# Counting a graph's edges in groups of three tiles and windows of 32 instead of five and 48

## The chip, the core and the metric

The kernel runs on one core of a Trainium2 chip. The metric is the device time of one execution in microseconds (us), lower being better. The core's engines run programs of their own and meet at semaphores: TensorE (PE) for matmuls and transposes, VectorE (DVE), ScalarE (ACT), GpSimd (POOL), and SyncE (SP), whose queue issues the DMAs. Matmuls write to PSUM, eight banks of 512 float32 columns; everything else lives in SBUF.

## The reference

Two graph attention layers over one graph of 1250 nodes and 21,250 edges (10,000 random pairs in both directions, and one loop per node), which come sorted by destination.

```
x = layernorm(x + gat0(x, src, dst))        # 12 heads of 64
x = layernorm(x + gat1(x, [src, dst]))      # 4 heads of 256, then 1 head of 768
# in each: e = leaky_relu(a1[src] + a2[dst]); w = exp(e - max over the edges of dst)
#          out[dst] = sum of w * ft[src] / sum of w, over the edges of dst
```

## The kernel before

Attention is computed densely: for every pair of nodes the kernel needs the number of edges between them, a matrix CT of 1250 x 1250 counts, held as ten tiles of 128 source nodes by 1250 destinations. Its logarithm (LC, in the same memory) is later added to the scores. So the first stage counts edges, and everything from the logarithms on waits for all counts.

**How edges are counted.** The edges make 170 tiles of 125. For each tile DVE builds two one-hot matrices: `hot_cell` (L1550, 125 edges x 480 columns) says in which of 10 x 48 cells the edge falls, the cell being the source's tile of 128 nodes and the destination's place in a window of 48 destinations; `hot_rows` (L1609, built for ten tiles in one operation, "the row op") says which of 128 rows the source is. PE multiplies the two (L759), and the product adds the tile's edges to a PSUM bank of 128 x 480 counts. Five tiles (GT) make a group with one window, since the edges are sorted; the group's window begins at its smallest destination, the base, which is data and is loaded into a register. There are 34 groups. Groups take turns on two banks, 0 and 4.

**How a group leaves its bank.** ACT copies columns 1 to 47 of each window over CT (L1214, `keep_window`); column 0, in which neighbouring groups may both have edges, is added to CT by DVE (L1562, `add`, 128 x 10 elements). Both load the base first (L1208 on ACT, L1566 on DVE). The last group is added whole by DVE, and that sets the semaphore `counted`.

**What orders it.** Every engine's order is written out by hand. PE may begin group g when `win_added` says that the add of group g-2 is done, so that its bank is free. DVE's order in group g is: one-hot tiles 0 and 1, the add of group g-2, the load of group g-1's base, tiles 2 and on. The add waits for PE to have finished group g-2 (`win_free`) and for ACT's copy of it (`win_kept`). A one-hot tile waits for the tile ten before it to be used, as there are ten `hot_cell` buffers.

**What PE and ACT do between.** PE interleaves the counting with the first layer's other work: transposes of x (L867) in 18 turns, with copies on ACT (L1243), and projections (L895) in 20 steps, with copies on ACT (L1263, L1265); in two places also transposes of attention rows (L881, copies L1254). `x_counts` and `proj_counts` say how many counting segments stand ahead of each turn or step. A segment is three or two tiles, and stands in an `If`, as another program runs if a group's destinations are spread too far for a window. Between two pieces of other work (four turns, or two steps) stand two groups. On ACT the copies of the groups stand at the same places.

## Time and profile before

| what | us |
|---|---|
| median of 3 runs | 1126.23 |
| lowest and highest | 1125.57, 1126.36 |
| the profiled execution | 1124.05 |
| its span, first to last instruction | 1122.3 |
| counting, first one-hot tile to `counted` | 11.6 to 79.0 |

The profile is of one execution. Its own time, 1124.05, is the span and 1.75 around it. Over the whole span PE is busy 94%, DVE 85% and ACT 57%. The three thirds of the kernel have different limits, so what a change in the counting does must be read from the stretch up to 79 us and from what waits for its end.

### The profile page before, as it was taken

To read this page: it belongs to the slowest core of one execution; us is meant where nothing else is said; L and a number is where in the kernel's file an instruction comes from. 1 tells how busy PE (TensorE), PEld (TensorE's weight loads), DVE (VectorE), ACT (ScalarE), POOL (GpSimd) and SP (SyncE) were. 2 spreads that over 40 slices of the span, in tenths; PEclk is the share of its full clock that TensorE was granted. 3 is DMA by queue.
4 is the path that set the end of the run, shared out by engine and by line. 5 is a ranking of instruction groups with operands and counts; after the bars stand their busy time and mean duration, and the time that the engine had idled before them with its cause. 6 is when DMAs were issued, how large, how long until landed. Compare 5 with 4: busy or idle time off the path is not lost.

```text
span 1122.3 us, 20577 instructions
## 1 busy us (share of the span) xinstructions
PE 1052.4 (94%) x8048; PEld 905.6 (81%) x8048; DVE 952.9 (85%) x1531; ACT 642.5 (57%) x939; POOL 142.6 (13%) x155
## 2 busy tenths in 40 slices
PE   6986999898989899999999999999999999999996
PEld 4665666666666667999999999999988888888885
DVE  7989999999999999977853999999987874497865
ACT  8658999999999997223111567666612311234331
POOL 1000000000000000010073112020400153311111
PEclk9998999999999999999999999999999999999998
DMA  4061020202020205533237310204041124343211
GB/s 150 1 235 44 3 92 1 93 1 92 2 92 1 98 1 197 171 101 120 80 107 267 124 47 1 84 1 151 20 169 57 44 95 174 131 162 126 78 60 53
DMA packets 40022, 98.99 MB, mean 88 GB/s; under 512 B 4505, under 2 KB 17393, under 8 KB 39925
## 3 DMA queue, kind: packets, MB, share of 16 engines
q1 hardware_dynamic: 39926, 97.66, 24.9%
q8 instruction: 66, 1.08, 0.4%
q14 instruction: 30, 0.25, 0.1%
HBM read 70.74 MB, written 26.90 MB: 87 GB/s over the span
## 4 chain that ended last, share of the span: by engine, by line
PE 61%; DVE 20%; ACT 9%; issue 8%; DMA 1%; DVEq 1%; POOL 0%; SPq 0%; POOLq 0%; ACTq 0%
PE psum L1110 14%; PE psum L1019 13%; PE psum L1071 12%; DVE R L1692 9%; PE psum L1149 8%; DVE R L1678 5%; ACT R L1288 5%; PE psum L1034 4%; ACT R L1304 3%; PE psum L759 2%; PE psum L1087 1%; PE psum L944 1%; DVE LC L1664 1%; PE psum L1140 1%; PE psum L1122 1%
## 5 line engine op out<-in xcount | busy, mean ns | idle before, releaser
L944 PE MATMUL psum<-ident,R 128*128 128x128 f32 (+3 forms) x1200 | 156.8, 279 | 38.3 <-ACT R L1288 37.8
L944 PEld LDWEIGHTS psum<-ident,R 128*128 128x128 f32 (+3 forms) x1200 | 127.5, 142 | 78.9 <-ACT R L1288 66.5
L1692 DVE CUSTOM_DVE_ANT_0 R<-R,LC 128x1250 f32<-128x1250 f32 x120 | 175.1, 1462 | 0.2 <-DVE LC L1664 0.2
L1288 ACT ACTIVATE R<-R,row_max 128x1250 f32<-128x1250 f32 x120 | 161.6, 1347 | 2.0 <-DVE row_max L1692 1.6
L958 PE MATMUL psum<-R 128*64 128x256 f32 (+3 forms) x1200 | 147.2, 383 | 0.6 <-ACT R L1304 0.6
L1304 ACT COPY R<-psum 128x1280 f32<-128x1280 f32 x120 | 143.7, 1198 | 1.5 <-PE psum L944 1.5
L1019 PE MATMUL psum<-w_hi,x1T_hi 128*128 128x256 f32 (+1 forms) x480 | 128.6, 283 | 0.7 <-DVE x1T_lo L1784 0.7
L1019 PE MATMUL psum<-w_hi,x1T_lo 128*128 128x256 f32 (+1 forms) x480 | 127.3, 280 | 0.0
L1019 PE MATMUL psum<-w_lo,x1T_hi 128*128 128x256 f32 (+1 forms) x480 | 125.7, 281 | 0.0
L1678 DVE SCALAR_TENSOR_TENSOR R<-R 128x1250 f32<-128x1250 f32 x80 | 121.9, 1525 | 0.0
L2177 POOL TENSOR_TENSOR rstd<-rstd,minus_half 128x1 f32<-128x1 f32 (+1 forms) x40 | 33.9, 847 | 664.1 <-DVE rstd L1707 664.1
L958 PEld LDWEIGHTS psum<-R 128*64 128x64 f32 (+1 forms) x1200 | 79.0, 137 | 43.6 <-issue 10.1
L1019 PEld LDWEIGHTS psum<-w_hi,x1T_hi 128*128 128x128 f32 (+1 forms) x480 | 86.6, 186 | 1.3 <-issue 1.3
L1019 PEld LDWEIGHTS psum<-w_hi,x1T_lo 128*128 128x128 f32 (+1 forms) x480 | 86.3, 186 | 0.0
L1019 PEld LDWEIGHTS psum<-w_lo,x1T_hi 128*128 128x128 f32 (+1 forms) x480 | 85.4, 186 | 0.1
L1375 ACT CAST et_hi<-psum 128x1280 fp32r<-128x1280 f32 (+1 forms) x40 | 48.2, 1206 | 56.6 <-PE psum L1034 56.6
L1367 ACT ACTIVATE R<-R,row_max 128x1250 f32<-128x1250 f32 (+1 forms) x40 | 53.7, 1342 | 33.3 <-DVE row_max L1846 33.2
L1983 DVE TENSOR_TENSOR h1T_lo<-psum,h1T_hi 128x1024 fp32r<-128x1024 f32 (+1 forms) x18 | 21.8, 1209 | 54.8 <-ACT h1T_hi L1403 54.8
L1403 ACT CAST h1T_hi<-psum 128x1024 fp32r<-128x1024 f32 (+1 forms) x18 | 18.1, 1006 | 81.6 <-PE psum L1087 81.6
L1924 DVE TENSOR_TENSOR et_lo<-psum,et_hi 128x1280 fp32r<-128x1280 f32 (+1 forms) x40 | 58.2, 1455 | 7.1 <-ACT et_hi L1375 5.7
L1678 DVE SCALAR_TENSOR_TENSOR R<-rowbuf,R 128x1250 f32<-128x1250 f32 (+1 forms) x40 | 60.7, 1523 | 0.0
L1846 DVE CUSTOM_DVE_ANT_0 R<-R,LC 128x1250 f32<-128x1250 f32 (+1 forms) x40 | 58.7, 1468 | 0.1
(234 smaller groups left out, 2482.9 us busy)
## 6 DMA issues: line engine op xcount, KB each, us to landing
R<-rows_spill SPq DMA_DIRECT2D x20, 625.0 KB, 5.2
rowbuf<-rows_spill SPq DMA_DIRECT2D x14, 625.0 KB, 5.2
lc_spill<-LC SPq DMA_DIRECT2D x9, 625.0 KB
LC<-lc_spill SPq DMA_DIRECT2D x9, 625.0 KB, 5.6
res_spill<-colbuf SPq DMA_DIRECT2D x36, 128.0 KB, 3.3
R<-res_spill SPq DMA_DIRECT2D x9, 512.0 KB, 3.5
R<-in_x_dram SPq DMA_DIRECT2D x1, 3456.0 KB
res_spill<-R SPq DMA_DIRECT2D x9, 384.0 KB
```

What stands on the lines that cost most here:

```text
L944: last = e.transpose(turn0[r % 2][0:m, s, 0:n_dst], ring[0:n_dst, r % RING0, s * P:s * P + m], ident[0:n_dst, 0:n_dst])
L958: last = e.matmul(banks[6][k * C0:(k + 1) * C0, 0:w], x_in[0:m, s, (2 * g + k) * C0:(2 * g + k + 1) * C0], exp_bufs0[(2 * n + k) % 4][0:m, ...
L1019: last = e.matmul(gemm_bank1(p)[0:m, 0:C1], xs[:, i * KT + k, 0:m], ws[b % WBUFS1][:, k, :], start=(n == 0), stop=(n == len(steps) - 1))
L1071: last = e.matmul(acc1[r % 2][0:w, :], cols[r % 2][0:m, s, 0:w], xs[h % 2][0:m, s, :], start=(s == 0 and step == 0), stop=(s == NT - 1 and ...
L1110: last = e.matmul(acc2[v % 2][0:m, c:c + w], hs[v % 2][:, k, 0:m], ws[k][:, c:c + w], start=(k == 0 and step == 0), stop=(k == KH - 1 and ...
L1149: last = e.matmul(acc2[r % 2][0:n_dst, c:c + w], cols[r % 2][0:m, s, 0:n_dst], xs[s][0:m, c:c + w], start=(s == 0 and step == 0), stop=(s ...
L1288: e.activation(ring[0:m, r % RING0, :], ring[0:m, r % RING0, :], ACT.Exp, bias=row_max[0:m, r % RING:r % RING + 1], scale=-1.0, accum_out= ...
L1304: e.copy(exp_bufs0[(2 * n + j // 2) % 4][:, :, (j % 2) * P:(j % 2) * P + rows[i]], turn0[r % 2][:, :, 0:rows[i]]).then_inc(S.kept0, 1)
L1678: e.scalar_tensor_tensor(out=ring[0:m, r % RING0, :], in0=row_slope[0:m, :], scalar=att_part0[0:m, i, H0 + h:H0 + h + 1], in1=row[0:m, :], ...
L1692: e.tensor_tensor_reduce(slot, slot, LC[0:m, i, :], -1.0, MIN_CEILING, ALU.add, ALU.min, row_max[0:m, r % RING:r % RING + 1]).then_inc(S.l ...
L1846: e.tensor_tensor_reduce(slot1(r)[0:m, :], slot1(r)[0:m, :], LC[0:m, i, :], -1.0, MIN_CEILING, ALU.add, ALU.min, row_max[0:m, r % RING:r % ...
L1924: e.tensor_tensor(et_lo[r % 2][:, :, 0:w], turn1[r % 2][:, :, 0:w], et_hi[r % 2][:, :, 0:w].bitcast(F32), ALU.subtract).then_inc(S.et_lo, 1)
```

## The change

Groups are of three tiles, with windows of 32 destinations: 57 groups, of which the last has two tiles. A one-hot tile has 10 x 32 = 320 columns, and so has its matmul; ACT's copy has 310 elements per row. The number of `hot_cell` buffers stays ten, and the row op still makes ten tiles. A segment is now one group. Between two pieces of PE's other work stand three groups (nine tiles) instead of two (ten tiles); ahead of the first transposes seven groups (21 tiles) instead of four (20), and after the last projection eight groups (23 tiles) instead of three (15). Because 57 groups of three are not 170 tiles, the destinations that give the bases are loaded by two DMAs, and the subtraction of the bases is two operations.

```diff
-    GT = 5
-    GROUPS = ET // GT
-    WIN = 48
+    GT = 3
+    GROUPS = (ET + GT - 1) // GT
+    WIN = 32
...
-        HOT = 2 * GT
+        HOT = 10
...
-            e.dma_start(groups_i, dst.rearrange("(g e) -> g e", g=GROUPS)).then_inc(S.groups_in, 16)
+            e.dma_start(groups_i[0:KEPT, :], dst[0:KEPT * GT * EP].rearrange("(g e) -> g e", g=KEPT)).then_inc(S.groups_in, 16)
+            e.dma_start(groups_i[KEPT:GROUPS, :], dst[E - GT * EP:E].rearrange("(g e) -> g e", g=1)).then_inc(S.groups_in, 16)
...
-        def windows_pe(e, g, tiles):
-            if g >= 2 and tiles[0] == 0:
+        def group_tiles(g):
+            return range(g * GT, min(g * GT + GT, ET))
+
+        def windows_pe(e, g):
+            if g >= 2:
                 e.wait_ge(S.win_added, g - 1)
-            for j in tiles:
-                e.wait_ge(S.win_hot, g * GT + j + 1)
-                hot_row = hot_rows[g // 2 % 2][:, :, g % 2 * GT + j]
-                e.matmul(banks[4 * (g % 2)][:, 0:NT * WIN], hot_row, hot_cell[(g * GT + j) % HOT], start=(j == 0),
-                         stop=(j == GT - 1)).then_inc(S.win_free, 1)
+            tiles = group_tiles(g)
+            for t in tiles:
+                e.wait_ge(S.win_hot, t + 1)
+                hot_row = hot_rows[t // PAIR % 2][:, :, t % PAIR]
+                e.matmul(banks[4 * (g % 2)][:, 0:NT * WIN], hot_row, hot_cell[t % HOT], start=(t == tiles[0]),
+                         stop=(t == tiles[-1])).then_inc(S.win_free, 1)
...
-        SEGMENTS = [range(0, 3), range(3, GT)]
-        COUNTS = len(SEGMENTS) * GROUPS
-        W_COUNTS, FIRST_COUNTS, TURN_COUNTS = 2, 8, 26
+        W_COUNTS, FIRST_COUNTS, TURN_COUNTS, STEP = 2, 7, 22, 3
 
         def x_counts(turn):
-            return FIRST_COUNTS + turn // 4 * 2 * len(SEGMENTS)
+            return FIRST_COUNTS + turn // 4 * STEP
 
         def proj_counts(pair):
-            return TURN_COUNTS + pair // (2 * KG) * 2 * len(SEGMENTS)
+            return TURN_COUNTS + pair // (2 * KG) * STEP
...
             for g in range(GROUPS):
-                if g and g % 2 == 0:
-                    rows_of_pair(g // 2)
-                for j in range(GT):
-                    tile(g * GT + j)
+                for j, t in enumerate(group_tiles(g)):
+                    if t and t % PAIR == 0:
+                        rows_of_pair(t // PAIR)
+                    tile(t)
                     if g >= 2 and j == 1:
                         add(g - 2, base)
                     if g and j == 1:
...
-            e.tensor_tensor(by_group(dst_rel), by_group(banks[0][0:EP, 0:ET]),
-                            base_all.unsqueeze(2).to_broadcast([EP, GROUPS, GT]), ALU.subtract).then_inc(S.prep, 1)
+            for to, node, base in zip(by_group(dst_rel), by_group(banks[0][0:EP, 0:ET]), bases_by_group()):
+                e.tensor_tensor(to, node, base, ALU.subtract).then_inc(S.prep, 1)
```

PE's order in the projection stretch, from the end of the first group of a block to the next projection, before (`win_hot_ready` is set by DVE's one-hot tiles, `win_sum_added` is `win_added`):

```order
L822 UNCONDITIONAL_BRANCH
L822 COMPARE_AND_BRANCH
L759 MATMUL psum<-R 128x480 [waits win_hot_ready,win_sum_added]
L759 MATMUL psum<-R 128x480 [waits win_hot_ready] x2
L822 UNCONDITIONAL_BRANCH
L822 COMPARE_AND_BRANCH
L759 MATMUL psum<-R 128x480 [waits win_hot_ready] x2
L822 UNCONDITIONAL_BRANCH
L895 MATMUL psum<-R 128x66 [waits ft]
```

The same place after the change, from the end of the first group of a block:

```order
L825 UNCONDITIONAL_BRANCH
L825 COMPARE_AND_BRANCH
L765 MATMUL psum<-R 128x320 [waits win_hot_ready,win_sum_added]
L765 MATMUL psum<-R 128x320 [waits win_hot_ready] x2
L825 UNCONDITIONAL_BRANCH
L825 COMPARE_AND_BRANCH
L765 MATMUL psum<-R 128x320 [waits win_hot_ready,win_sum_added]
L765 MATMUL psum<-R 128x320 [waits win_hot_ready] x2
L825 UNCONDITIONAL_BRANCH
L898 MATMUL psum<-R 128x66 [waits ft]
```

A third group, with a wait of its own for an add, now stands ahead of the projection.

DVE's order around one row op, before (L1562 ISA computes an address for the add and carries its waits; `win_rest_kept` is `win_kept`, `win_hot_free` is `win_free`):

```order
L1550 TENSOR_SCALAR R<-R 125x480 [waits win_hot_free] x3
L1609 TENSOR_TENSOR R<-R 125x1280
L1550 TENSOR_SCALAR R<-R 125x480 [waits win_hot_free] x2
L1562 ISA [waits win_sum_added,win_rest_kept,win_hot_free]
L1562 TENSOR_TENSOR LC<-LC,psum 128x10
L1566 TENSOR_LOAD R
L1566 ISA x2
L1550 TENSOR_SCALAR R<-R 125x480 [waits win_hot_free] x5
```

The same after the change:

```order
L1557 TENSOR_SCALAR R<-R 125x320 [waits win_hot_free] x3
L1569 ISA [waits win_sum_added,win_rest_kept,win_hot_free]
L1569 TENSOR_TENSOR LC<-LC,psum 128x10
L1573 TENSOR_LOAD R
L1573 ISA x2
L1616 TENSOR_TENSOR R<-R 125x1280
L1557 TENSOR_SCALAR R<-R 125x320 [waits win_hot_free] x3
L1569 ISA [waits win_sum_added,win_rest_kept,win_hot_free]
```

Add, load and their waits now stand behind every three tiles instead of every five, and the row op falls at changing places in the groups.

## Rows read from the trace of the kernel before

**Rows 1.** Busy us of each engine (instructions) by stretch, granted clock, DMA
```profile
core 0: us, PE busy (x) PEld busy (x) DVE busy (x) ACT busy (x) POOL busy (x), PEclk, DMA share, GB/s
22.00:36.00 14.00, 12.95 (x87) 10.16 (x85) 14.00 (x54) 10.10 (x22) 0.00 (x0) 1.00 0.01 2
79.10:360.00 280.90, 246.78 (x2008) 179.84 (x2008) 280.60 (x297) 256.58 (x351) 0.00 (x0) 0.98 0.14 49
```

**Rows 2.** Instructions in time: start, duration, engine, operation, idle before; a projection-stretch block
```profile
45.41 2.25 PE L759 MATMUL psum<-R 125*128 125x480 bf16 x10
...
46.19 0.16 DVE L1562 TENSOR_TENSOR LC<-LC,psum 128x10 f32 x1
46.27 1.34 DVE L1550 TENSOR_SCALAR R<-R 125x480 bf16<-125x480 f16 x5
...
46.76 0.56 ACT L1214 COPY LC<-psum 128x470 f32 x1 [0.68 <-PE psum L759]
47.54 0.16 DVE L1562 TENSOR_TENSOR LC<-LC,psum 128x10 f32 x1
...
47.59 1.56 PE L895 MATMUL psum<-R 64*128 64x66 f32 x24
...
48.17 0.85 DVE L1550 TENSOR_SCALAR R<-R 125x480 bf16<-125x480 f16 x3 [0.47 <-PE psum L759]
```

**Rows 3.** The same view, the counting's start
```profile
11.98 2.21 PE L759 MATMUL psum<-R 125*128 125x480 bf16 x5 [3.46 <-DVE R L1550]
...
15.32 0.56 ACT L1214 COPY LC<-psum 128x470 f32 x1 [0.18 <-PE psum L759]
...
16.11 0.17 DVE L1562 TENSOR_TENSOR LC<-LC,psum 128x10 f32 x1 [0.65 <-PE psum L759]
...
16.76 0.60 DVE L1550 TENSOR_SCALAR R<-R 125x480 bf16<-125x480 f16 x2 [0.48 <-PE psum L759]
...
17.16 0.14 PEld L759 LDWEIGHTS psum<-R 125*128 125x128 bf16 x1 [0.32 <-DVE R L1550]
```

**Rows 4.** Waits from 16 to 79.2 us: us in total, times, longest
```profile
PEld psum L759 <- DVE LC L1562: 4.4, 10, 0.7
```

**Rows 5.** Groups by line up to 130 us: busy us, mean ns of one, idle before
```profile
L1550 DVE TENSOR_SCALAR R<-R 125x480 bf16<-125x480 f16 x170 | 47.3, 338 | 4.7 <-PE psum L759 3.4 <-issue 1.0
...
L1609 DVE TENSOR_TENSOR R<-R 125x1280 bf16<-125x1280 f16 x17 | 13.9, 819 | 0.0
```

**Rows 6.** In order of time: the transposing stretch, its first and last transposes
```profile
19.33 1.67 PE L867 MATMUL psum<-ident,R 128*128 128x128 f32 x14
...
20.06 1.82 ACT L1243 COPY R<-psum 128x512 f32<-128x512 f32 x4
...
20.84 2.20 PE L759 MATMUL psum<-R 125*128 125x480 bf16 x10
...
33.28 0.80 PE L867 MATMUL psum<-ident,R 128*128 128x128 f32 x6
```

**Rows 7.** In order of time: the first and the tenth pair of projections
```profile
36.27 1.56 PE L895 MATMUL psum<-R 64*128 64x66 f32 x24
...
71.70 1.41 PE L895 MATMUL psum<-R 64*128 64x66 f32 x24
```

**Rows 8.** In order of time: the block behind the first row transposes
```profile
57.60 2.20 PE L759 MATMUL psum<-R 125*128 125x480 bf16 x10
...
59.29 0.53 ACT L1214 COPY LC<-psum 128x470 f32 x1
```

**Rows 9.** In order of time: the end of the counting
```profile
73.04 3.24 PE L759 MATMUL psum<-R 125*128 125x480 bf16 x12
...
75.45 0.17 DVE L1562 TENSOR_TENSOR LC<-LC,psum 128x10 f32 x1
...
79.07 0.28 DVE L1757 TENSOR_SCALAR R<-att 128x240 f32<-128x240 f32 x1
```

**Rows 10.** DVE's base loads, line L1566: times, ns min/median/max, first and last start
```profile
L1566 DVEq TENSOR_LOAD <-R x34: 297/304/942, 11.8 to 76.5; - x34
```

More of the change, by code:

```diff
@@ L53, in gnn_kernel @@
     RING = 8
-    GT = 5
-    GROUPS = ET // GT
-    WIN = 48
+    GT = 3
+    GROUPS = (ET + GT - 1) // GT
+    WIN = 32
     KEPT = GROUPS - 1
     HT = NT // 2
-    assert GROUPS * GT == ET and GROUPS % 2 == 0 and NT % 2 == 0 and NT * WIN <= BANK
+    assert KEPT * GT < ET and NT % 2 == 0 and NT * WIN <= BANK
     x1_dram = nc.dram_tensor("x1_spill", (N, D), F32, kind="Internal").ap()
@@ L168, in gnn_kernel @@
         RHS_AT = NT * D + 4 * P
-        hot_at = [RHS_AT + KT * PROJ + j * (NT * WIN // 2) for j in range(GT + 1)]
-        assert hot_at[GT] <= NT * (D + XW)
-        hot_cell = [edge_view([NT * WIN], BF16, EP) for _ in range(GT)]
-        hot_cell += [view(R2, at, [NT * WIN], BF16, EP) for at in hot_at[0:GT]]
-        PAIR = 2 * GT
+        hot_at = [RHS_AT + KT * PROJ + j * (NT * WIN // 2) for j in range(HOT // 2 + 1)]
+        assert hot_at[HOT // 2] <= NT * (D + XW)
+        hot_cell = [edge_view([NT * WIN], BF16, EP) for _ in range(HOT // 2)]
+        hot_cell += [view(R2, at, [NT * WIN], BF16, EP) for at in hot_at[0:HOT // 2]]
+        PAIR = HOT
         hot_rows = [edge_view([P, PAIR], BF16, EP) for _ in range(2)]
@@ L187, in gnn_kernel @@
         groups_i = edge_view([GT * EP], I32, GROUPS)
-        assert iota_at <= 4 * N and edge_at[0] >= 6 * N
+        edge_at[0] = max(edge_at[0], 6 * N)
+        assert iota_at <= 4 * N
         hot_full = [edge_view([N], BF16, EP) for _ in range(2)]
@@ L818, in pe_program, with count_group @@
             e.sem_inc(S.all_free, 2)
-            def count_segment(n):
-                g, part = divmod(n, len(SEGMENTS))
+            def count_group(g):
                 with e.If(span < WIN):
-                    windows_pe(e, g, SEGMENTS[part])
-                if n == 0:
+                    windows_pe(e, g)
+                if g == 0:
                     with e.Else():
@@ L828, in count_segment @@
                         last.then_inc(S.win_free, ET)
-                if n == COUNTS - 1:
+                if g == GROUPS - 1:
                     with e.Else():
@@ L834, in count_until @@
                 for at in range(done, n):
-                    count_segment(at)
+                    count_group(at)
                 return max(done, n)
@@ L899, in pe_program @@
                     turn_rows(n)
-            count_until(done, COUNTS)
+            count_until(done, GROUPS)
             e.wait_ge(S.counted, 1)
@@ L1216, in keep_until @@
             def keep_until(kept, counts):
-                for g in range(kept, min(counts // len(SEGMENTS), KEPT)):
+                for g in range(kept, min(counts, KEPT)):
                     keep_window(g)
-                return max(kept, min(counts // len(SEGMENTS), KEPT))
+                return max(kept, min(counts, KEPT))
             kept = keep_until(0, W_COUNTS)
@@ L1268, in act_program @@
                     keep_rows(n)
-            keep_until(kept, COUNTS)
+            keep_until(kept, GROUPS)
             for s in range(NT):
@@ L1543, in by_group, with bases_by_group @@
         def by_group(per_tile):
-            return per_tile.rearrange("p (g t) -> p g t", t=GT)
+            return [per_tile[:, 0:KEPT * GT].rearrange("p (g t) -> p g t", t=GT), per_tile[:, KEPT * GT:ET].unsqueeze(1)]
+        def bases_by_group():
+            return [base_all[:, 0:KEPT].unsqueeze(2).to_broadcast([EP, KEPT, GT]),
+                    base_all[:, KEPT:GROUPS].unsqueeze(2).to_broadcast([EP, 1, ET - KEPT * GT])]
         def windows_dve(e, rows_of_pair):
@@ L1581, in all_dve @@
         def all_dve(e):
-            e.tensor_tensor(by_group(dst_f), by_group(dst_rel), base_all.unsqueeze(2).to_broadcast([EP, GROUPS, GT]),
-                            ALU.add).then_inc(S.prep, 1)
+            for to, rel, base in zip(by_group(dst_f), by_group(dst_rel), bases_by_group()):
+                e.tensor_tensor(to, rel, base, ALU.add).then_inc(S.prep, 1)
             e.tensor_copy(src_f, src_i).then_inc(S.prep, 1)
-            e.wait_ge(S.prep, PREP_CELL + 2)
+            e.wait_ge(S.prep, PREP_CELL + 3)
             for g in range(HT):
```

8 lines of the change are left out of this document (4 added, 4 removed).

## The prediction

> **What bounds the kernel now.** I read three views in this order: the busy time by stretch, the waits of the counting stage, and the instructions in order of time. From 22 to 36 us DVE is busy 14.0 of 14.0 us and PE 12.95 [rows 1]: no engine has much to spare there. After the counting, from 79.1 to 360 us, DVE is busy 280.6 of 280.9 us [rows 1], on work that needs all counts: whatever the counting gains or loses is passed on whole.
>
> The stage is a three-engine loop over two PSUM banks. PE may begin group g only when DVE has added group g-2's first column; DVE does that after two one-hot tiles of group g, and only when ACT has copied group g-2 out. Behind each such add, DVE's queue loads the next window's base, and no later tile starts before it has. When the add had to be waited for, the next tile starts 0.63 us after it (47.54 to 48.17) or 0.65 (16.11 to 16.76); when it had been free early, 0.08 (46.19 to 46.27) [rows 2, 3].
>
> Before, PE does two groups between two pieces of other work. Both need adds of the previous block's groups, which DVE makes while PE is at the other work. So the loop seldom stops PE: its longest list of waits for those adds sums to 4.4 us [rows 4].
>
> **The work that shrinks.** A one-hot tile has 320 columns, not 480. At 338 ns for 480 [rows 5], 160 columns are worth between 0 (all of it fixed) and 0.113 us (none of it); back to back the tiles start 0.255 apart (five in 46.27 to 47.54 [rows 2]), and I take 0.04, since most of so short an op is fixed cost. For 170 tiles that is 6.8 us of DVE (bounds 0 and 19). Against it stand 23 more adds at 0.08: 1.8. Ten matmuls take 2.20 us [rows 6], one alone 0.37, so they start 0.203 apart; with a third of the columns gone 0.137 (bound: 0.203, no gain), 11 us of PE. ACT's copy of 470 elements takes 0.56 [rows 2]; for 310 I take 0.42, between 0.37 (in proportion) and 0.56. All this would pay if either engine's work set the pace.
>
> The Trainium skill (VectorE: DVE Perf Modes, errata section) says that ops reading SBUF pay a fixed extra latency each and that small tiles pay it per tile. The 0.16 us of the ten-element add at 46.19 agrees [rows 2]. [...]
>
> **The wait that is added.** After the change PE does three groups a, b, c between two pieces of other work. Group c needs the add of a, which is of the same block. So inside each block stands this chain, from the block's first matmul:
>
> - a's three matmuls, to the start of ACT's copy: before, 1.35 us for five (45.41 to 46.76) [rows 2]. Two spacings go (0.41), two shrink by 0.07, and so does the last matmul: 0.74.
> - the copy 0.42, and 0.20 from its end to the add (15.32 + 0.56 to 16.11 is 0.23 [rows 3]; I take a little less, as that add had one more condition).
> - DVE's queue stood at that wait, so the base load is exposed: 0.64 to the third tile of c.
> - from that tile's start to its matmul: 0.40 (16.76 to 17.16) [rows 3], less 0.04: 0.36.
> - from the last matmul to PE's other work: of ten matmuls from 45.41 (the first spacing 0.05 longer, since the row is 2.25 where another is 2.20) the last starts at 47.28, and L895 at 47.59 [rows 2, 6]: 0.31, less 0.07 for the shorter matmul: 0.24.
>
> That is 2.60 us. Queued behind DVE's waiting add are c's third tile and the next block's first tiles; PE waits for the former. The adds of b and c have slack: they fall into PE's other work.
>
> **Projection stretch** (L895, from 36.27, the tenth at 71.70: 35.4 us for nine periods) [rows 7]. A projection row lasts 1.56 and the next matmul overlaps it by 0.07: 1.49. A period is then 4.09. Two periods also hold row transposes with their copies on ACT: in the first, ACT is only free for the block's copy at 59.29, 1.69 after the first matmul at 57.60 [rows 8] where the chain has 0.74, and the transposes take 0.9; the second costs 0.4. One period has the one-hot row op right ahead of c's third tile: 0.82 [rows 5] less 0.08 of overlap. 9 x 4.09 + 0.95 + 0.9 + 0.4 + 0.74 = 39.8: plus 4.4.
>
> **Transposing stretch** (L867, 19.33 to 33.28: 13.95 us for four periods) [rows 6]. Fourteen transposes take 1.51 (19.33 to 20.84). ACT has x copies until 21.88, 1.04 after the block's start [rows 6], and can start the next op a little earlier, so copy a comes 0.15 to 0.3 later; I take 0.2. A period is 2.60 + 0.2 + 1.51 = 4.31, one with twelve transposes 0.2 less: 17.0, plus 3.1. From the last transposes to the first projection it was 2.99 (33.28 to 36.27) [rows 6, 7]; now 0.65 + 2.60 + 0.1: plus 0.4.
>
> **Start.** ACT's clearing lets the first copy start at 15.32 [rows 3]. That stays; the shorter copy puts the first add at 15.95. But by then only groups 0 and 1 are through, six tiles where ten were. From there two groups cost one round of the loop: 0.64 + 0.36 + 0.42 (matmul to copy) + 0.42 + 0.20 = 2.04. Two rounds bring the add of group 4 to 20.0; the row ops ahead of tiles 10 and 20 add 0.74 each, then 0.36 and 0.25: transposes from 22.1 instead of 19.33, plus 2.8. The preparation (one more DMA, reductions over 375 instead of 625 elements, one more subtraction) costs nothing: DVE can be over 1 us late before tile 8 is missed. If that cover were gone it would be some 0.4.
>
> **End.** After the last projection came 15 tiles and now come 23, in eight groups. Before: 73.04 to 79.07, 6.03 us [rows 9]. Now 1.36 to the first add, five more adds each a group apart, and what follows the last add of the loop (75.45 to 79.07, 3.62 [rows 9], less 0.17 for the shorter last add and 0.4 for fewer tiles). A group costs DVE's queue the 0.64 and three tiles and the next wait, about 1.0 with a base load of 0.30 us; but loads took up to 0.94, under the store traffic of this stretch [rows 10], so 1.0 to 1.6. I take 1.25, since the stores are further along when the end comes later. 1.36 + 6.25 + 3.05 = 10.7: plus 4.6, bounds 3.4 and 6.4.
>
> **Sum.** 2.8 + 3.1 + 0.4 + 4.4 + 4.6 = 15.3 us. The profiled execution took 1124.05 us (span 1122.3), so 1139.4 for its like; the median of the runs shown is 1126.23, 2.2 above it, so I forecast 1141.5. Per block 0.1 less (each term at its lower row) to 0.3 more, over 15 blocks, with the end's bounds and a start later by up to 3: plus 11 to plus 24.
>
> **Rivals.** (1) *Work sets the pace, and it is faster*: DVE's 6.8 - 1.8 = 5.0 us come off the stage: 1121.2. For it: DVE full from 22 to 36 us [rows 1]. Against it: an add cannot precede its copy, nor the copy its matmul; this decides only if the chain of 2.6 us took less than the block's own nine tiles of DVE, some 1.9. Chance 0.08. (2) *The base load is hidden*: c's third tile starts 0.08 after the add, 0.55 less in some 20 rounds: plus 4 to 5, 1131. Against it: a load stands behind the add in DVE's queue, and the queue takes nothing out of turn in the rows. Chance 0.07. (3) *TensorE's clock*: it was granted in full from 22 to 36 us [rows 1]. The first five matmuls of the trace take 2.21 us [rows 3], 0.40 apiece and double the later 0.203: 1.2 GHz, though the clock column reads 1.00 there; before them PE had done almost nothing. PE now idles about two of the four us before 16, so the lower clock may stay longer: some 3 us (inside my bounds). If it kept falling through the stage, the 1.5 of other work would double and the chain grow by 0.5: 2.0 us in each of 15 periods, plus 30 on top, 1172. Chance 0.05. The Trainium skill (TensorE: Matmul & The Clock Gate, on the clock gate) has the clock fall on idling and rise on sustained matmuls; by that rule it is this thinning that would bring 1172, and no row here shows a stretch thinned like this one. (4) *The windows do not hold*: the program then counts every tile over all nodes, five times 170 tiles each above the 0.34 us of a 480-column one: over 290 us instead of 67, above 1345. The inputs' widest group of 375 edges spans 25 nodes, the clipped last one 31, under 32: chance 0.01.
>
> **Numbers.** Forecast, plus 11 to plus 24: 0.79. The range 1131 to 1151 takes in (2). Within 0.2% (about what a measurement of this kernel can tell from no change) lie only mixtures of (1) and (2), 0.03. Faster 0.08, same 0.03, slower 0.89.
>
> **What would show it.** In the changed profile: PE waits for DVE's adds over 10 us in all; from ACT's copy to the add 0.2, from the add to the next tile about 0.64 once per block; projections 4.1 us apart; first transposes near 22 us; the all-counts add ends near 94 to 95 us instead of 79; after it everything as before, only later. Projections less than 3.9 apart, or counting over before 85, would make the forecast wrong; so would a granted clock below 1.0 between 20 and 90 us.

## The result and the profile after

The changed kernel is slower: 1158.6 us at the median, against 1125.5 for the kernel before in the same set of runs. The ratio is 1.0276 (95% interval 1.0255 to 1.0297), some 31 us. Forecast were 1141.5 us and a range of 1131 to 1151: the direction was right, the size half of what came, and the range too low. (A sixth run of the changed kernel, disturbed and 3586.7 us long, counts in the median, which is 1158.3 without it, but not in the ratio.)

The profiled execution took 1161.1 us, its span is 1159.4. The profile shows the first news in its line of the TensorE clock. These are the profile's head and two of its lines of 40 slices, 29 us each, in tenths:

```profile
span 1159.4 us, 20867 instructions
...
DVE  4655999999999999996883699999987865387865
...
PEclk9755899999999999999999999999999999999998
```

Before, no slice of the clock stood under 8 in the whole kernel; now the second to fourth, 29 to 116 us, stand at 7, 5 and 5. The stretches, in the same columns as [rows 1], show its two levels:

```profile
29.00:46.00 17.00, 12.57 (x84) 9.08 (x82) 12.62 (x53) 10.68 (x26) 0.00 (x0) 1.00 0.01 1
46.00:84.00 38.00, 35.61 (x207) 23.61 (x206) 18.84 (x78) 16.14 (x46) 0.00 (x0) 0.51 0.01 1
84.00:90.00 6.00, 4.56 (x51) 3.50 (x50) 4.45 (x18) 3.22 (x10) 0.00 (x0) 1.00 0.07 11
90.00:117.00 27.00, 22.48 (x117) 13.17 (x115) 16.00 (x62) 8.81 (x25) 0.00 (x0) 0.51 0.70 255
118.00:400.00 282.00, 248.33 (x2018) 179.96 (x2016) 280.59 (x297) 259.57 (x356) 0.00 (x0) 0.98 0.12 39
```

For 64 of the 71 us from 46 to 117, TensorE ran at 1.2 GHz, its lower level. In the kernel before only the stage's first matmuls show that level [rows 3]. DVE, full from 22 to 36 us before [rows 1], works half of the time. Behind the stage it is full again, as it was (280.6 of 282.0).

The five marks of the stage, in order of time (answering [rows 6, 7, 9]), say where the time went:

```profile
23.51 3.14 PE L870 MATMUL psum<-ident,R 128*128 128x128 f32 x14
...
42.26 0.80 PE L870 MATMUL psum<-ident,R 128*128 128x128 f32 x6
...
46.77 2.83 PE L898 MATMUL psum<-R 64*128 64x66 f32 x24
...
100.39 2.55 PE L898 MATMUL psum<-R 64*128 64x66 f32 x24
...
114.56 2.32 PE L914 MATMUL psum<-ident,LC 128*98 128x128 f32 x10 [1.11 <-DVE LC L1569]
```

| Stretch | before, us | forecast | after |
|---|---|---|---|
| to the first transposes | 19.33 | +2.8 | +4.2 |
| first to fifth transposes | 13.95 | +3.1 | +4.8 |
| to the first projections | 2.99 | +0.4 | +1.5 |
| first to tenth projections | 35.43 | +4.4 | +18.2 |
| tenth projections to the turn of the counts (L914) | 7.39 | +4.6 | +6.8 |
| sum | 79.09 | +15.3 | +35.5 |

Behind L914 the kernel before takes 1043.2 us of its span, this one 1044.8: the rest is only shifted, as forecast. (This profiled execution is the longest of five; they ran from 1151.1 to 1161.1 us, with mean granted clocks of 0.980 to 0.963 in that order, so that the part of the clock in +35.5 is a little more than usual.)

One block at the full clock up to its last matmul, which answers [rows 2]:

```profile
44.00 1.01 PE L765 MATMUL psum<-R 125*128 125x320 bf16 x6 [0.95 <-DVE R L1557]
...
44.72 0.42 ACT L1217 COPY LC<-psum 128x310 f32 x1 [0.99 <-PE psum L765]
45.34 0.17 DVE L1569 TENSOR_TENSOR LC<-LC,psum 128x10 f32 x1 [0.49 <-PE psum L765]
...
45.57 0.49 PE L765 MATMUL psum<-R 125*128 125x320 bf16 x2 [0.55 <-DVE LC L1569]
45.99 0.73 DVE L1557 TENSOR_SCALAR R<-R 125x320 bf16<-125x320 f16 x3 [0.48 <-PE psum L765]
46.35 0.48 PE L765 MATMUL psum<-R 125*128 125x320 bf16 x1 [0.30 <-DVE R L1557]
```

It is the chain that was forecast, link by link: copy 0.72 after a's first matmul (forecast 0.74), add 0.62 later (0.62), tile 0.65 later (0.64), its matmul 0.36 later (0.36), and the projections at 46.77, 0.42 later (0.24). But the row of that last matmul is 0.48 long, where the others of its kind take 0.35: the clock was falling there. Where it was in full again, the last link is 0.28:

```profile
88.98 0.35 PE L765 MATMUL psum<-R 125*128 125x320 bf16 x1 [0.52 <-DVE R L1557]
89.26 1.61 PE L898 MATMUL psum<-R 64*128 64x66 f32 x24
```

Then the same block at half the clock:

```profile
49.53 1.81 PE L765 MATMUL psum<-R 125*128 125x320 bf16 x6
...
50.67 0.42 ACT L1217 COPY LC<-psum 128x310 f32 x1 [0.47 <-PE psum L765]
51.28 0.17 DVE L1569 TENSOR_TENSOR LC<-LC,psum 128x10 f32 x1 [2.15 <-PE psum L765]
...
51.94 0.73 DVE L1557 TENSOR_SCALAR R<-R 125x320 bf16<-125x320 f16 x3 [0.49 <-issue]
...
52.71 2.83 PE L898 MATMUL psum<-R 64*128 64x66 f32 x24
```

The copy comes 1.14 after the first matmul, not 0.72, and a pair of projections takes 2.76 (46.77 to 49.53) instead of 1.49. The period is 5.94 (52.71 less 46.77), where 4.09 was forecast and 3.94 stood before on the average of nine.

### The profile page after: what moved, and what is told of

It reads as the page before. It is cut to its first block, busy times and chain, and to the rows that moved or that the text cites. A ratio compares the mean times of both kernels' runs of the same rounds, so it can differ in the third digit from the quotient of the medians.

```text
span 1159.4 us, 20867 instructions
## 1 busy us (share of the span) xinstructions
PE 1077.9 (93%) x8048; PEld 919.2 (79%) x8048; DVE 949.5 (82%) x1555; ACT 647.9 (56%) x962; POOL 145.0 (13%) x155
## 3 DMA queue, kind: packets, MB, share of 16 engines
q8 instruction: 66, 1.08, 0.4%
## 4 chain that ended last, share of the span: by engine, by line
PE 61%; DVE 17%; ACT 11%; issue 8%; DVEq 1%; POOL 1%; DMA 0%; POOLq 0%; ACTq 0%
PE psum L1113 14%; PE psum L1022 12%; PE psum L1074 12%; PE psum L1152 8%; DVE R L1699 7%; DVE R L1685 5%; ACT R L1291 5%; PE psum L1037 4%; ACT R L1307 3%; PE psum L765 2%; PE psum L898 2%; PE psum L947 1%; PE psum L1090 1%; PE psum L1143 1%; PE psum L1125 1%
## 5 line engine op out<-in xcount | busy, mean ns | idle before, releaser
L765 PE MATMUL psum<-R 125*128 125x320 bf16 x170 | 52.0, 431 | 19.5 <-DVE LC L1569 9.7
```

The source lines that it names most:

```text
L765: e.matmul(banks[4 * (g % 2)][:, 0:NT * WIN], hot_row, hot_cell[t % HOT], start=(t == tiles[0]), stop=(t == tiles[-1])).then_inc(S.win_fre ...
```

## The experiments

Fifteen kernels ran. "Counts" is when L914 (L911 in the kernel before), the first transposes of the finished counts, starts in the profiled execution. Medians of different sets of runs differ by their sets too, so a difference between two kernels is safer by their ratios to the kernel before.

| Kernel | median us | ratio to before (95%) | counts at | mean clock of the profiled run |
|---|---|---|---|---|
| before (five sets of runs) | 1125.5 to 1126.6 | 1 | 79.1 | 0.992 |
| changed | 1158.6 | 1.0255 to 1.0297 | 114.6 | 0.963 |
| e1_three_banks | 1136.1 | 1.0075 to 1.0109 | 88.4 | 0.985 |
| e2_busy_waits | 1148.6 | 1.0186 to 1.0220 | 102.3 | 0.986 |
| e3_early_base | 1139.3 | 1.0108 to 1.0142 | 91.3 | 0.988 |
| e4_gt3_win48 | 2097.2 | 1.8584 to 1.8649 | other branch | 0.978 |
| e4_win48 | 1152.8 | 1.0228 to 1.0270 | 106.5 | 0.988 |
| e5_spread | 1147.0 | 1.0139 to 1.0271 | 93.4 | 0.986 |
| e6_gt5_win32 | 1118.6 | 0.9923 to 0.9957 | 71.8 | 0.990 |
| e7_before_banks_base | 1126.4 | 0.9993 to 1.0012 | 78.4 | 0.990 |
| e8_banks_base | 1130.4 | 1.0025 to 1.0052 | 84.0 | 0.985 |
| e9_tail_no_loads | 1128.0 | 1.0010 to 1.0029 | 81.5 | 0.993 |
| e10_gt4_win36 | 1118.3 | 0.9923 to 0.9950 | 73.1 | 0.987 |
| e11_two_per_block | 1155.1 | 1.0244 to 1.0275 | 107.6 | 0.966 |
| e12_fill_start | 1163.8 | 1.0312 to 1.0347 | 112.8 | 0.968 |
| e13_fill_blocks | 1150.9 | 1.0194 to 1.0229 | 103.1 | 0.985 |
| e14_gt4_two_banks | 1131.8 | 1.0032 to 1.0066 | 85.5 | 0.989 |

### Is it the chain? e1, e3, e5

Three banks, adds three groups late:

```
-            if g >= 2:
-                e.wait_ge(S.win_added, g - 1)
+            if g >= 3:
+                e.wait_ge(S.win_added, g - 2)
-                e.matmul(banks[4 * (g % 2)][:, 0:NT * WIN], hot_row, ...
+                e.matmul(banks[(0, 4, 1)[g % 3]][:, 0:NT * WIN], hot_row, ...
-                    if g >= 2 and j == 1:
-                        add(g - 2, base)
-                    if g and j == 1:
-                        base = base_of(g - 1)
+                    if g >= 3 and j == 1:
+                        add(g - 3, base)
+                    if g >= 2 and j == 1:
+                        base = base_of(g - 2)
```

> The changed kernel, but its groups take turns in three PSUM banks instead of two, and VectorE adds group g-3's first column (not g-2's) ahead of group g's third tile; to free the third bank the first three row turns share one bank. No group of a block then needs an add of its own block. Theory A (the loss is the chain inside the block, and the low TensorE clock is its consequence, since TensorE stands still in that chain): PE's waits for adds shrink from 20 us or more to under 5, the granted clock stays 1.00 from about 20 us to the end of the counting, projections come about 3.0 to 3.5 us apart instead of 5.9, and the time is 1116 to 1126 us. Rival B (fewer columns in each matmul thin TensorE's work, and that alone lowers the clock): waits shrink, but the clock is at half for 40 us or more of the stage: 1132 to 1145. Rival C (57 groups instead of 34 cost the time by themselves, in adds, base loads and copies): 1145 or more, no matter how many banks.

Measured: 1136.1, above the range of A and below that of C; it lies in B's, but the full clock (below) is not what B expected. The two rows of waits for adds, from 16 to 115 us in the changed kernel and to 110 here (columns as [rows 4]; the first is the weight load, the second the matmul):

```profile
PEld psum L765 <- DVE LC L1569: 20.1, 26, 2.4
...
PE psum L765 <- DVE LC L1569: 9.7, 20, 2.3
```

```profile
PEld psum L765 <- DVE LC L1569: 12.2, 26, 1.8
...
PE psum L765 <- DVE LC L1569: 4.6, 13, 1.3
```

The clock stays in full from 22 to 79 us, and nine periods of projections take 33.6 us (40.02 to 73.61) where the kernel before takes 35.4. The chain is gone and the block with it; but 14.8 us follow the tenth projections instead of 7.4. That is another cause (e9).

The base load ahead of the wait:

```
                     if g and j == 1:
-                        base = base_of(g - 1)
+                        next_base = base_of(g - 1)
+                        if g >= 2:
+                            add(g - 2, base)
+                        base = next_base
```

> The changed kernel with one edit: VectorE loads the next window's base before it waits for the add, not behind the add. Theory A with the chain as forecast (the base load stands exposed, 0.5 to 0.64 us in each round whose add was waited for, some 25 to 30 rounds): the tile behind a waited-for add starts 0.1 to 0.2 us after it instead of 0.6 to 0.65, and the time falls by 11 to 17 us, to 1140 to 1147; more if the clock comes back with the shorter waits. Rival D (what stands there is not the load but TensorE, whose freed ring slot the tile waits for, or a fixed cost behind every wait): the tile still starts 0.5 or more after the add and the time stays within 4 us of the changed kernel's 1157.

Measured: 1139.3, 17 us less than the changed kernel by the ratios and 19 by the medians, from one line moved. A waited-for add and its tile, in order of time:

```profile
52.62 0.17 DVE L1569 TENSOR_TENSOR LC<-LC,psum 128x10 f32 x1 [0.24 <-issue]
52.71 0.72 DVE L1557 TENSOR_SCALAR R<-R 125x320 bf16<-125x320 f16 x3
...
52.85 0.35 PEld L765 LDWEIGHTS psum<-R 125*128 125x128 bf16 x3 [0.91 <-DVE LC L1569]
```

The tile starts 0.09 after the add instead of 0.65, and a period of projections is 3.70 (53.41 less 49.71). So the load was the exposed link, and rival D falls. At the full clock that is 0.52 us a block (4.22 in e2, below); the total lies at or above the upper end of the 11 to 17 expected, and the clock came back as well, in full from 29 to 84 us.

TensorE's other work behind every group instead of every three:

```
-            return FIRST_COUNTS + turn // 4 * STEP
+            return FIRST_COUNTS + turn * STEP // 4
-            return TURN_COUNTS + pair // (2 * KG) * STEP
+            return TURN_COUNTS + pair * STEP // (2 * KG)
```

> The changed kernel with two banks and everything else as it is, but TensorE's other work (transposes, projections) is cut so that a third of it stands behind every single group instead of all of it behind three. Theory A: between group a and group c now lie two groups and two thirds of the other work, about 1.8 us, longer than the 1.4 us from a's first matmul to its add; PE's waits for adds fall below 6 us, the clock stays in full, ten projections take 33 to 37 us instead of 56 and the time is 1132 to 1142. What is left over 1126 would be the start and the eight groups of the end. Rival C (57 groups cost it wherever they stand): 1150 or more.

Measured: 1147.0, but in two pairs: 1140.0 and 1139.6 with mean clocks of 0.986 and 0.988, 1153.9 twice with 0.972. At the full clock it lands where A put it; TensorE's waits for adds are 5.5 and 10.5 us where under 6 was expected. The two pairs are the same code with the clock lost or not: 14 us.

### Is it the clock? e2, e12, e13

The changed kernel, with dummy matmuls of zeros ahead of the waits:

```
             if g >= 2:
+                extra = 8 if g == 2 else 4 if g < FIRST_COUNTS else 5 if (g - FIRST_COUNTS) % STEP == STEP - 1 else 0
+                for _ in range(extra):
+                    e.matmul(banks[5][:, 0:NT * WIN], zeros[:, 0:P], zeros[:, 0:NT * WIN], start=True, stop=True)
                 e.wait_ge(S.win_added, g - 1)
```

> The changed kernel with its two banks, its chain and its waits, but TensorE does dummy matmuls of zeros (320 columns, into a bank nobody reads) while it would wait for an add: eight ahead of group 2, four each ahead of groups 3 to 6, five ahead of the third group of every block. Theory A: the waits stay about as long as in the forecast (4.1 us from one projection to the next), but the clock is granted in full from about 20 us on, so only the chain's price is left: 1137 to 1144 us, the stage ending near 95 us. Rival C (the number of groups costs it, the clock is a bystander): within 3 us of the changed kernel's 1157. If the dummies only add work: 1160 or more.

e12 and e13 have the 8 and 4 alone, and the 5 alone:

> The changed kernel with dummy matmuls in its start only: eight ahead of group 2, four each ahead of groups 3 to 6, none in the blocks. If the late rise of the clock (29 us) decides: it rises by 17 to 20 us and stays in full until 90 us or later, and the time is 1147 to 1151, as with dummies everywhere. If the waits inside the blocks decide: it rises early but is at half again for 30 us or more between 35 and 100 us, and the time is 1152 to 1160.

> The changed kernel with five dummy matmuls ahead of the third group of every block and none in the start. If the waits inside the blocks decide: the clock rises late (24 to 29 us) but is then in full but for a few us until the last projection, and the time is 1148 to 1152. If the late rise decides: it falls again before 60 us and the time is 1153 or more.

(All three also let the row transposes share one bank, as the dummies need the other.)

Measured: 1148.6, 1163.8 and 1150.9. From 46 to 84 us, e2, then e12, then e13:

```profile
46.00:84.00 38.00, 33.62 (x298) 23.83 (x296) 23.95 (x101) 20.53 (x62) 0.00 (x0) 0.91 0.09 23
```

```profile
46.00:84.00 38.00, 34.81 (x202) 22.57 (x200) 17.77 (x73) 15.81 (x45) 0.00 (x0) 0.50 0.01 1
```

```profile
46.00:84.00 38.00, 33.61 (x315) 24.74 (x314) 24.98 (x103) 21.37 (x62) 0.00 (x0) 0.96 0.07 17
```

Work that does nothing made the kernel 8 us faster by the ratios, 10 by the medians, and it is the dummies in the blocks that do it. Those of the start gave the full clock earlier (the first fourteen transposes take 1.67 us instead of 3.14), 0.6 us in all, and then, with no dummies in the blocks, it was lost at 41 us; by the medians the kernel is 5 us slower than the changed one (it also has the shared bank, which costs e2 a wait of 1.16 us). e2 is above the 1137 to 1144 that A expected: its nine periods from projections to projections are 4.22, 4.48, 4.21, 4.21, 4.80, 8.24 (with the row transposes), 4.80, 4.22 and 4.27, where I had 4.09 and 3.0 for the three odd ones together. That is the forecast's own sum at (nearly) the full clock, and it comes to +23.2, not +15.3: by the stretches of the table +3.6, +3.4, +1.4, +8.0 and +6.8. It is an upper figure. In the period of 8.24 TensorE waits 1.16 us for the shared bank, e2's own edit, and loses its clock behind that wait (six matmuls in 1.80, which take 1.03 at the full clock):

```profile
70.10 1.01 PE L887 MATMUL psum<-ident,att 128*6 128x128 f32 x4 [1.16 <-ACT rowbuf L1260]
70.91 1.80 PE L768 MATMUL psum<-R 125*128 125x320 bf16 x6
```

e13 has the same wait and a shorter stretch at the lower clock, and its period is 7.16 (68.56 to 75.72). Without the wait and this difference of 1.08 the projections would be some +5.8 and the sum +20.9, an estimate from these rows. In e2's end two sets of dummies stand in the way, and the granted clock is 0.76 from 96 to 102 us.

### Columns or groups? e4, e6

The changed kernel with wider windows:

```
-    WIN = 32
+    WIN = 48
```

> The changed kernel with windows of 48 again (480 columns in each tile, matmul and copy), groups of three and three per block as they are: the number of columns alone undone. Theory A (waiting lowers the clock): the chain is longer (copies 0.56 instead of 0.42, matmuls 0.203 instead of 0.137 apart at full clock), TensorE waits as much, the clock still falls, and the time is 1160 to 1172. Rival B (the thinner matmuls lower the clock): the clock is granted in full, as before the change, and the time is 1144 to 1152, below the changed kernel although there is more work.

It took the other branch: with windows of 48 the last ones, pushed back to fit, reach over their neighbours, and every tile is then counted over all nodes. It priced my fourth rival, 2097 us, and told nothing else. With the branch made always true as well:

```
-                with e.If(span < WIN):
+                with e.If(span < N):
```

> The changed kernel with windows of 48 again (480 columns in each tile and matmul, 470 in each copy), groups of three and three per block as they are: the number of columns alone undone. The branch on the windows' width is made always true, since with 48 the last windows are pushed back over earlier ones and the counts there come out wrong; only its time is read. Theory A (waiting lowers TensorE's clock): the chain is 0.3 us longer per block, TensorE waits for adds as long as in the changed kernel, its clock is at half for 30 us or more of the counting, and the time is 1155 to 1170. Rival B (the thinner matmuls lower the clock): the granted clock is 1.00 through the stage, as before the change, and the time is 1140 to 1150, below the changed kernel's 1158 although there is more work.

Measured: 1152.8 us, with the clock in full:

```profile
46.00:84.00 38.00, 30.78 (x267) 19.54 (x264) 26.53 (x98) 23.44 (x59) 0.00 (x0) 1.00 0.02 3
```

Theory A expected 1155 to 1170 and a clock at half, B 1140 to 1150 and a clock in full: B on the clock, neither on the time. TensorE is busy in 31 of 38 us and keeps its clock; the changed kernel lost it after 12.57 of 17. (Its time is not clear of the changed kernel's: the intervals overlap.) So my sentence "waiting lowers the clock" is too simple: the same waits with wider matmuls between them do not. Nor do thin matmuls alone, in the kernel before (the branch always true again):

```
-    WIN = 48
+    WIN = 32
```

> The kernel before with one edit: 32 columns per window instead of 48, groups still of five, two per block (columns alone changed). Five tiles span more than 32 nodes, so the branch is made always true and counts beyond the window come out wrong; only its time is read. If the thinner work pays as forecast (a tile 0.04 us shorter, 6.8 us of VectorE, the copies 0.14 shorter): the counting ends at 73 to 76 us instead of 79 and the time is 1119 to 1124. Rival B (the thinner matmuls thin TensorE's work so that its clock falls): the clock is at half for 20 us or more between 20 and 90 us, and the time is over 1130. Rival E (the stage isn't paced by the tiles' length): within 2 us of the kernel before.

Measured: 1118.6 us, faster than the kernel before by 0.4 to 0.8%, clock in full, counts at 71.8 instead of 79.1. The thinner work pays 7.3 us, the 6.8 and a little of the forecast.

The three together, by the start of L914: columns alone -7.3, groups and blocks alone +27.4 (e4_win48), sum +20.1; both at once +23.2 with the dummies (e2) and +35.5 without them. Of these only both at once lose the clock.

### The end, and a third question: e8, e9, e11

The edits of e1 and e3 in one kernel:

> The changed kernel with both edits: three banks with adds three groups late, and the base load ahead of the wait for the add. With three banks alone VectorE still stood at some adds with a base load exposed behind. Theory A, in its second form (once no chain is left, the counting is paced by VectorE's own work: three tiles 0.645, an add 0.17 and a third of a row op 0.25 for each of 57 groups, 61 us, from 16 us on): projections 3.2 to 3.4 us apart, first transposes near 20.5, last projection near 72, then the end with its eight groups at about 1.5 us each (base loads of 0.95 us under the stores): first turn of the counts at 84 to 87 us against 88.4 with three banks alone, time 1130 to 1134. If exposed bases no longer matter there: 1135 to 1137.

Measured: 1130.4, projections from 38.63 to 70.66 (3.56 a period with the row transposes, 2.9 to 3.5 without), counts at 84.0: as expected. The end is the rest of the loss.

And e1 without the base loads of the end:

```
             def base_of(g):
+                if g >= 46:
+                    return 20 * g
                 return e.value_load(...)
```

(the same for ScalarE's copies)

> The changed kernel with three banks, and for the last eleven groups the bases are constants of the program on VectorE and ScalarE, so that no base is loaded there (their counts land in wrong columns; only the time is read). Theory: in the kernel with three banks every group of the end costs 1.6 us, of which the base load takes 0.95 while the stores of the residual run, and three loads in a row stand ahead of the last three adds. Without them a group costs 0.9 to 1.1 and the last adds follow at once: the end shrinks from 13.6 to 6.5 to 9 us, and the time from 1136 to 1129 to 1132. Rival: ScalarE's copies or the tiles' ring pace the end, not the loads: 1134 or more.

Measured: 1128.0, below the expected range. First the base loads of the kernel with three banks in its end (its line L1573; times, ns min/median/max, first and last start), and its last adds; then the last adds without loads:

```profile
L1573 DVEq TENSOR_LOAD <-R x8: 299/947/1321, 75.7 to 86.2; - x8
```

```profile
83.65 0.17 DVE L1569 TENSOR_TENSOR LC<-LC,psum 128x10 f32 x1
83.97 0.42 ACT L1217 COPY LC<-psum 128x310 f32 x1 [1.14 <-PE psum L765]
87.07 0.17 DVE L1569 TENSOR_TENSOR LC<-LC,psum 128x10 f32 x1 [3.26 <-issue]
```

```profile
79.24 0.16 DVE L1569 TENSOR_TENSOR LC<-LC,psum 128x10 f32<-128x10 f32 x1
79.32 0.72 DVE L1557 TENSOR_SCALAR R<-R 125x320 bf16<-125x320 f16 x3
...
79.96 0.47 DVE L1569 TENSOR_TENSOR LC<-LC,psum 128x10 f32<-128x10 f32 x2
```

A load that takes 0.30 us elsewhere takes 0.95 while the stores of the residual move 410 GB/s, and each group has one on DVE and one on ACT. With them a group of the end costs 1.6 us (adds at 80.43, 82.02, 83.65), without them 0.71 (78.53, 79.24). Before, the end held three groups, with loads of 0.76 us at the median of four; now eight. Part of what e9 gains may be the clock: from 84 to 90 us, at its end, e1 has it at 0.50 (its first turn of the counts takes 2.32 us), and e9 has it in full there (1.28).

The changed kernel with two groups per block:

```
-        ... TURN_COUNTS, STEP = 2, 7, 22, 3
+        ... TURN_COUNTS, STEP = 2, 7, 17, 2
```

> The changed kernel (groups of three, 32 wide, two banks) with two groups per block instead of three: no group then needs an add of its own block, but 22 groups are left behind the last projection instead of eight. Theory A: PE waits little for adds in the blocks, the clock stays in full until the last projection, projections are 2.5 to 2.8 us apart, the last ends near 60 us; then 22 groups at 1.0 us each, 1.6 where the stores run, and the counts are complete at 84 to 92 us: 1130 to 1139. Rival C (the groups cost it wherever they stand): 1150 or more. If the clock falls in the long end, where TensorE does little: up to 1145.

Measured: 1155.1, a plain miss. The clock fell here too, at 40 us, with nobody in a block waiting for an add of the same block. Just before, from 36 to 40, TensorE was busy 2.37 of 4 us, with 1.20 of standing still for a one-hot tile:

```profile
29.00:46.00 17.00, 14.37 (x110) 11.61 (x108) 12.20 (x50) 11.07 (x30) 0.00 (x0) 0.82 0.01 1
46.00:84.00 38.00, 35.07 (x270) 25.09 (x269) 20.77 (x86) 20.53 (x61) 0.00 (x0) 0.68 0.26 90
```

and the 22 groups left over took the 30 us from 77 to 107.

### What beats both: e7, e10, e14

The edits of e1 and e3 in the kernel before:

> The kernel before (groups of five, 48 wide, two per block) with the two edits that helped the changed kernel: a third PSUM bank with adds three groups late, and the next base loaded ahead of the wait for an add. Theory A: PE waits 4.4 us for adds in the kernel before, most of it in the start, where bases also stand exposed; up to 4 us are to be had: 1120 to 1125. Rival: VectorE's work paces the stage as it is, and nothing is gained: 1125 to 1127. Slower than 1128 would mean that later adds collide with the end of the stage, where three adds and three base loads now stand behind the last tile.

Measured: 1126.4, no change: the kernel before is paced by DVE's work, and taking its waits gives nothing.

The edits of e10 are those of e1 and e3 and these:

```
-    GT = 3
-    WIN = 32
+    GT = 4
+    WIN = 36
-            return FIRST_COUNTS + turn // 4 * STEP
+            return FIRST_COUNTS + turn // 4 * STEP // 2
```

(with 2, 5, 17 and 5 for the first, the start's, the turn's groups and the step, and the same halving for the projections).

> What the runs point to, as one version: groups of four tiles, 36 wide (43 groups), in turn two and three groups per block, three banks, bases loaded ahead of the adds; in the inputs the widest four tiles span 32 to 34 nodes. By VectorE's work (four tiles 0.90, an add 0.17, four tenths of a row op 0.33: 1.40 for each of 43 groups, 60 us, against 63 for the kernel before): the counting ends at 76 to 78 us instead of 79 and the time is 1121 to 1125, a little under the kernel before. If the end with its four or five groups and their slow base loads eats it: 1125 to 1129. If TensorE's clock falls in places: 1130 or more.

Measured: 1118.3 us, ratio 0.9923 to 0.9950: faster than both kernels, better than expected. In 16 to 36 us DVE is busy in 19.63 of 20, as full as in the kernel before [rows 1], and its tiles are shorter (0.307 us against 0.338):

```profile
16.00:36.00 20.00, 17.76 (x142) 15.63 (x142) 19.63 (x84) 15.91 (x42) 0.00 (x0) 1.00 0.12 41
```

e14 is e10 without the edits of e1 and e3:

> Groups of four, 36 wide, in turn two and three per block, as in the version that beat both kernels (1118.3), but with the two banks, the adds two groups late and the base loads behind the adds, as the kernels shown have them. If the group size and the shorter blocks carry the gain: a block with three groups has 12 tiles, 3.6 us of VectorE's work, longer than the chain of some 3 us, so that little is lost: 1119 to 1124. If the gain came from the removed waits: 1127 to 1140, with PE waiting over 10 us for adds.

Measured: 1131.8, with 4.9 and 11.8 us of waits for adds: between the two ranges, nearer the second. The 13 us between e14 and e10 (13.5 by the medians, 12.6 by the ratios) are the banks and the early base together, since nothing else differs. In the kernel before the same two edits gave nothing (e7), and in groups of four they decide between a loss and a gain: thinner work shows only where the loop's waits don't take its place.

## Why the prediction came out as it did

**The chain: right, and right in size.** A plain period at the full clock lasts 4.22 us in e2, against 4.09. In the block at 44.00 four of the five links were right to 0.02 us. The fifth, from the last matmul to the other work, is 0.28 at the full clock and not 0.24: the shorter matmul takes off 0.03, not the 0.07 that I took. Behind projections the first link is 0.80 (46.11 to 46.91 in e2) and not 0.74, as ACT is at the projections' copies until 46.77. The sizes of the thinner work were right too: a tile takes 0.299 us at the median, 0.04 less, and a copy 0.42. e3 takes the exposed base load away and the link goes from 0.65 to 0.09.

**The stretches: each too small, 7.9 us in all by e2, some 5.6 without what e2 itself adds.** The sum of 15.3 failed first as a sum at the full clock, where e2 measured 23.2. The start was +3.6 for 2.8. The transposes were +3.4 for +3.1. From the last transposes to the first projections it was +1.4 for +0.4: TensorE stands 0.95 us for a tile there, which waits for a row op (the row at 44.00 above). The projections were +8.0 for +4.4: 2.2 of the excess is e2's own, 1.2 is nine periods of 4.22 instead of 4.09, and 0.3 a row op ahead of a tile of another group than c. The forecast's 1.85 for the first row transposes was about right (1.72 in e3, 61.35 to 66.77 against 3.70). The end was +6.8 for +4.6, and its bounds (3.4 to 6.4) did not hold. I had put a group there between 1.0 and 1.6 us by the base load alone and taken 1.25. The changed kernel's adds of the end come 1.44 apart (104.97 to 113.61, six spacings): its loads are mostly quiet by then (0.31 us at the median of nine), as I argued with the stores being "further along", but TensorE is at half its clock. Where the end comes earlier, at the fuller clock, the loads are slow instead (e2: 0.84 at the median; e1: 0.95), and the end is as long. What the loads of these groups cost is shown by e9, in the kernel with three banks: 8.0 us from the tenth projections to the counts (73.53 to 81.49) where e1 has 14.8.

**The clock: the step that failed.** Rival (3) had the mechanism, its sign, and nearly its price: 4.09 + 2.0 = 6.1 us for a period, measured 5.94. It had the chance of 0.05, an all-or-nothing form (1172) and no term in the sum. It came true for 64 us of the stage and is worth 12.3 us in the profiled execution (35.5 less 23.2), 10 by the medians (1158.6 and 1148.6) and 8 by the ratios, each with e2's own 2 us counted against it. I gave it so little because the trace of before showed the clock full through the stage. But that row was of a TensorE busy in 12.95 of 14 us, and my own forecast put a wait into every block: the row spoke of another kernel. And the rule of the Trainium skill (TensorE: Matmul & The Clock Gate, "What's actually happening") that I had set against the change got a chance too small to move the range. The range, cut off at 1151, left this rival out. With the clock mostly kept and every mis-sized stretch in place, e2 (1148.6) and e13 (1150.9) lie inside it; with the stretches put right by 5.6 us and the clock lost, 1153 would still be outside. So the clock is what put the time out of the range, and the stretches had used up most of its room.

**Work sets the pace, faster (1): wrong here, right elsewhere.** e6 has the gain in full, 7.3 us where the columns were put at 6.8, in a loop without the chain; e10 has as much with 43 groups.

**The base load is hidden (2): wrong**; e3 is what that would have been, 1139.3 and not 1131. Of its 12.2 us to the counts over the kernel before, the end has 5.7 and the start 3.0.

**The windows (4): they held** in the changed kernel. The price of the other branch is 2097 us (e4_gt3_win48), far above the 1345 that I gave as its least.

**Forecast signs.** PE's waits for adds over 10 us in all: 9.7 and 20.1 by the two rows. Copy to add 0.2: yes. Transposes near 22: 23.5. Projections 4.1 apart: only at the full clock. Counts at 94 to 95: 114.6, 102.3 at the full clock. And "a granted clock below 1.0 between 20 and 90 us would make the forecast wrong" is what happened.

**Open.** What exactly costs the clock is not settled. e3 and e4_win48 stand still in 8.5 and 7.2 of the 38 us from 46 to 84 and keep it; e11 loses it at 40 us, and from 22 to 36 it had stood still for 1.8 us of 14; e5, by its mean clocks, loses it in two executions of four. Over stretches as long as these, busy time as the profile counts it does not rank the kernels. The falls of the three kernels come at one place, behind the last transposes, where TensorE waits for adds and for the tiles behind a row op: it was busy 2.37 us of 4 in e11 (36 to 40), 1.80 of 4 in e12 (38 to 42) and 3.25 of 6 in the changed kernel (40 to 46). Others pass that place and keep the clock. That filling the waits in the blocks restores it is shown (e2, e13); what the chip measures is not.

## What to carry to other kernels

When a stage's loop has N buffers, a block that puts N+1 rounds between two pieces of cover work puts the loop's whole round trip on the path: count the buffers before the work. Thinner pieces pay only after the waits are gone (e14 against e10, e6 against the change), and every piece has a price that does not shrink, here a register load of 0.3 to 0.95 us on two queues. If an edit both thins TensorE's work and adds waits, put the lower clock into the forecast as a case of its own with its price per period, even where the trace of before never shows it, and let the range reach it.

## What the runs showed of the hardware

- TensorE's clock fell to 1.2 GHz at 46 us in a stretch where it never stood still for longer than 0.95 us at a time (1.2 by its weight loads), busy in 12.57 of 17 us. The Trainium skill (TensorE: Matmul & The Clock Gate, "What's actually happening") has idling lower the clock and activity raise it. The trace agrees with the direction, and e2 and e13 confirm it, but none of the waits here was long: many short ones in thin work were enough, and in wider work (e4_win48) they were not.
- Dummy matmuls of zeros keep the clock: 104 of them, 20 us of TensorE's busy time, took 8 to 10 us off the kernel (e2 against the changed kernel); those at the start alone were worth nothing later (e12).
- A load of one register from SBUF takes 0.30 us at the median of every kernel's loads here (0.297 at the least), and 0.95 at the median, up to 1.32, while stores run at some 410 GB/s (e1, 76 to 86 us). The Trainium skill (DMA: Bandwidth & Descriptors, "Latency and other measured facts") gives `tensor_load` a floor of some 600 ns and does not say from which memory; the quiet rows here are half of that, and for a load from SBUF the measurement decides.
